# Folding the node mask into the last layer's relu in a four-layer graph network

## The chip, the cores and the metric

The kernel runs on one core of one Trainium2 chip. The metric is the device time of one execution in microseconds (us), as a median over runs. Five engines matter: TensorE (PE in the profile, with its weight loads as PEld), VectorE (DVE), ScalarE (ACT), GpSimd (POOL) and the DMA queue that SyncE (SP) feeds.

## What is computed

128 graphs of 128 nodes with 256 features pass four layers, each inside `x = layernorm(x + layer(x, adj))`. The layers are a hypergraph convolution with a hidden width of 512, a mean-aggregating layer, three stacked graph convolutions, and this last one, the only one whose code changes:

```python
def _L3_gnn_ref(x, a, kernel):
    t = jnp.einsum('bnm,bmf->bnf', a, x)
    out = jnp.einsum('bnf,fd->bnd', t, kernel)
    out = jax.nn.relu(out)
    mask = (jnp.sum((x != 0).astype(jnp.float32), axis=-1, keepdims=True) > 0).astype(jnp.float32)
    return out * mask
x = _layernorm(x + _L3_gnn_ref(x, adj, L3_gnn_kernel), axis=-1)
```

The mask has one number per node, 0 or 1.

## The kernel before, in words

The work unit is a pair of graphs: tiles are 128 partitions (nodes) by 2 x 256 elements. There are 64 pairs. The kernel is a software pipeline: `LAG` gives each stage the iteration in which it works, so that iteration n does, among others, stages R and P (layer one) of pair n-1, XAB and AXB (layer two) of pair n-2, Ax2, H1, H1W, H2 (layer three) of pair n-3, H2W, AP3, Ax3 and TK (end of layer three, and layer four) of pair n-4, and F (mask, last norm, store) of pair n-5. Each engine has its own hand-written order of operations in its function `body(n, k)`, and engines meet through counting semaphores alone. Iterations 0 to 2 are a written-out fill, and the last five drain the pipeline.

Products are made of three terms (hi x hi, hi x lo, lo x hi), so each operand is split in a rounded part (`_hi`, a copy on ScalarE, line 541) and a rest (`_lo`, a subtraction on VectorE, line 802, or on GpSimd, lines 1180 and 1188).

Names that the text uses:

- R writes the first layer's hidden values to PSUM; ScalarE's `relu_r` (line 565) makes `r_f`, `round_r` (541) `r_hi`, GpSimd's `low_r` (1188) `r_lo`; `square_r`, `add_squares` make `sq`, its halves and their sum. `copy_A` and `low_A` split the adjacency.
- A norm is `summed` (n_s), `stats` (n_st, 810), `mean_var` (n_mv, 815), `root` on ScalarE (n_std, 555), `invert` (n_rstd, 828), `shift` (n_shift, 832) and `apply` on ScalarE (560, two instructions, one per graph). The first norm is applied on VectorE instead (line 842). n1 to n4 are the norms of the four layers.
- `h_mean`, `h_var`, `h_veps`, `h_std`, `h_rstd` are the inner norm of layer one, and `p_f` (940) its result, which the matmuls of GP read.
- `x2c` (1265) is the second layer's result plus a bias, for the sum of the third (1108); `BH` (1207) serves the next pair's G; `h_lo` (1180) belongs to H1 and, later in the iteration, to H2.
- TK writes the last layer's product to PSUM bank 2. XAB of the next iteration writes the same bank, so TensorE waits there for `tk_relu` (line 379).
- F: VectorE counts the nonzero elements of `x3` and makes `mask` (1071, 1075). ScalarE has made `tk = relu(psum)` at the end of the iteration before (791, one 128x512 instruction). GpSimd multiplies `n4.s = tk * mask` first in its iteration (1246), and after `low_r`, `add_squares` and `low_A` adds `x3` (1254). VectorE's stats of n4 (line 1122) wait for that sum.

Of the kernel before, what the change touches and what calls it, by code (L numbers as in the profile page):

```python
# [7 lines left out]
ALU = mybir.AluOpType  # L8
ACT = mybir.ActivationFunctionType
# [8 lines left out]
           R=1, P=1, GP=1,  # L18
# [3 lines left out]
           F=5)  # L22
# [8 lines left out]
def build(nc, x, adjT, w1T, w2T, wab, v1, v2, v3, wk, columns, rows, eye, out):  # L31
    NP, C, GP_, D = x.shape
# [5 lines left out]
    with ExitStack() as ctx:  # L38
# [6 lines left out]
        def sem(name):  # L45
            return ctx.enter_context(nc.semaphore(name))
# [50 lines left out]
        x3 = sb("x3", [2, D])  # L97
# [51 lines left out]
        h1_relu, h1_hi, h1_lo, h1w_out = (sem(s) for s in ("h1_relu", "h1_hi", "h1_lo", "h1w_out"))  # L149
        h2_relu, h2_hi, h2_lo, h2w_hi, h2w_lo = (sem(s) for s in ("h2_relu", "h2_hi", "h2_lo", "h2w_hi", "h2w_lo"))  # L150
        x3_nz, mask_made = sem("x3_nz"), sem("mask_made")
        tk_masked = sem("tk_masked")
        ax3_hi, ax3_lo, tk_relu = sem("ax3_hi"), sem("ax3_lo"), sem("tk_relu")

        def begun(pair):

            return pair >= 0

        def upto(pair):

            return min(pair, NP - 1) + 1
# [5 lines left out]
        def active(stage, n):  # L167
            return 0 <= n - LAG[stage] < NP
# [25 lines left out]
        def bc(ap, shape, axis):  # L194
            return ap.unsqueeze(axis).to_broadcast(shape)
# [343 lines left out]
        def _(act):  # L539
# [44 lines left out]
            def round_r(n, k, h):  # L584
                p = n - 1
                act.wait_ge(r_relu[h], upto(p))
                if begun(p - 1):
                    act.wait_ge(pe_did["P"], upto(p - 1))
                copy(r_s[0][:, 2 * h:2 * h + 2], r_f[:, 2 * h:2 * h + 2]).then_inc(r_hi[h], 1)

            def square_r(n, k):
                p = n - 1
                act.wait_ge(r_relu[1], upto(p))
                if begun(p - 1):
                    act.wait_ge(sq_half, upto(p - 1))
                act.activation(sq[:], r_f[:], ACT.Square).then_inc(sq_made, 1)
# [104 lines left out]
            def body(n, k):  # L701
                if first(n, 4):
                    act.wait_ge(v_lo, 4)
                if active("x2", n):
                    p = n - 3
                    if begun(p - 1):
                        act.wait_ge(pe_did["Ax2"], upto(p - 1))
                        act.wait_ge(x2c_made, upto(p - 1))
                    apply(n2, p, x2)
                if active("R", n):  # L710
                    relu_r(n, k, 0)
                    relu_r(n, k, 1)
                if active("xT", n):
                    split_x1T(n, k)
                if active("R", n):
                    round_r(n, k, 0)
                if active("H2W", n):
                    split_hi("H2W", h2w, h2w_hi, n - 4, pe_did["AP3"])
                if active("R", n):
                    round_r(n, k, 1)  # L720
                if active("Ax2", n):
                    split_hi("Ax2", ax2, ax2_hi, n - 3, pe_did["H1"])
                if active("R", n):
                    square_r(n, k)
                    copy_A(n, k)
                if active("prep", n):
                    weight_column(n, k)
                if active("XAB", n):
                    out_XAB(n, k)
                if active("H1", n):  # L730
                    p = n - 3
                    act.wait_ge(pe_did["H1"], upto(p))
                    if begun(p - 1):
                        act.wait_ge(h1_lo, upto(p - 1))
                    relu_out("H1", 0, h1_f, c1_c)
                    relu_out("H1", 1, h1_f, c1_c).then_inc(h1_relu, 1)
                    act.wait_ge(h1_relu, upto(p))
                    if begun(p - 1):
                        act.wait_ge(pe_did["H1W"], upto(p - 1))
                    copy(h1_s[0][:], h1_f[:]).then_inc(h1_hi, 1)  # L740
                if active("AP3", n):
                    p = n - 4
                    root(n3, p)
                    if begun(p - 1):
                        act.wait_ge(pe_did["Ax3"], upto(p - 1))
                        act.wait_ge(n4.summed, upto(p - 1))
                        act.wait_ge(x3_nz, upto(p - 1))
                    apply(n3, p, x3)
                if active("F", n):
                    root(n4, n - 5)  # L750
                if active("P", n):
                    square_mean(n, k)
                if active("Tr", n):
                    copy_GT(n, k)
                if active("P", n):
                    root_h(n, k)
                if active("H1W", n):
                    p = n - 3
                    act.wait_ge(pe_did["H1W"], upto(p))
                    if begun(p - 1):  # L760
                        act.wait_ge(pe_did["H2"], upto(p - 1))
                    copy(h1w[:].rearrange("p g d -> p (g d)"),
                         psum[:, BANK["H1W"], 0:2 * D]).then_inc(h1w_out, 1)
                if active("Ax3", n):
                    split_hi("Ax3", ax3, ax3_hi, n - 4, pe_did["TK"])
                if active("Gx", n):
                    split_gx(n, k)
                if active("F", n):
                    p = n - 5
                    if p >= 2:  # L770
                        act.wait_ge(stored[p % 2], 16 * (p // 2))
                    apply(n4, p, x4[(k - 5) % 2])
                if active("H2", n):
                    p = n - 3
                    act.wait_ge(pe_did["H2"], upto(p))
                    if begun(p - 1):
                        act.wait_ge(h2_lo, upto(p - 1))
                    relu_out("H2", 0, h2_f, c2_c)
                    relu_out("H2", 1, h2_f, c2_c).then_inc(h2_relu, 1)
                    act.wait_ge(h2_relu, upto(p))  # L780
                    if begun(p - 1):
                        act.wait_ge(pe_did["H2W"], upto(p - 1))
                    copy(h2_s[0][:], h2_f[:]).then_inc(h2_hi, 1)
                if active("AXB", n):
                    root(n2, n - 2)
                if active("TK", n):
                    p = n - 4
                    act.wait_ge(pe_did["TK"], upto(p))
                    if begun(p - 1):
                        act.wait_ge(tk_masked, upto(p - 1))  # L790
                    act.activation(tk[:].rearrange("p g d -> p (g d)"), psum[:, BANK["TK"], 0:2 * D],  # L791
                                   ACT.Relu).then_inc(tk_relu, 1)
                if active("GP", n):
                    root(n1, n - 1)

# [382 lines left out]
        def _(pool):  # L1178
# [60 lines left out]
            def body(n, k):  # L1239
                if active("F", n):  # L1240
                    p = n - 5
                    pool.wait_ge(tk_relu, upto(p))
                    pool.wait_ge(mask_made, upto(p))
                    if begun(p - 1):
                        pool.wait_ge(n4.done, upto(p - 1))
                    pool.tensor_tensor(n4.s[:], tk[:], bc(mask[:], [C, 2, D], 2), ALU.mult).then_inc(tk_masked, 1)  # L1246
                if active("R", n):
                    low_r(n, k, 0)
                    low_r(n, k, 1)
                    add_squares(n, k)  # L1250
                    low_A(n, k)
                if active("F", n):
                    pool.wait_ge(tk_masked, upto(n - 5))
                    pool.tensor_tensor(n4.s[:], n4.s[:], x3[:], ALU.add).then_inc(n4.summed, 1)  # L1254
                if active("H1", n):
                    pool.wait_ge(h1_hi, upto(n - 3))
                    lo(h1_s, h1_f[:], h1_lo)
                if active("prep", n):
                    make_BH(n, k)
                if active("x2", n):  # L1260
                    p = n - 3
                    pool.wait_ge(n2.done, upto(p))
                    if begun(p - 2):
                        pool.wait_ge(n3.summed, upto(p - 2))
                    pool.tensor_tensor(x2c[(k - 3) % 2][:], x2[:], bc(c3_b, [C, 2, D], 1),
                                       ALU.add).then_inc(x2c_made, 1)
                if active("GP", n):
                    make_xb(n, k)
                if active("H2", n):
                    pool.wait_ge(h2_hi, upto(n - 3))  # L1270
                    lo(h2_s, h2_f[:], h2_lo)
# [44 lines left out]
```

## Time and profile before

| | |
|---|---|
| median of 3 runs | 1463.44 us (1463.33 to 1463.59) |
| the profiled execution's own time | 1463.48 us |
| its span, first to last instruction | 1461.7 us |
| granted TensorE clock, mean | 0.991 |
| busy share: PE, DVE, ACT, POOL | 97%, 74%, 72%, 58% |

A row of the timeline gives the start in us from the span's start, the duration in us, the engine, the line, the operation, what it writes and reads, and in brackets how long its engine sat idle before it and what ended that. Instructions of one kind that follow each other are merged ("x2"), and their duration is then from the first start to the last end. Neighbouring instructions of one engine overlap by about 0.05 to 0.1 us. Matmul ends are modelled, so a PE that looks busy without a break can still lose time between starts.

### The profile page before, as it was taken

How to read it: one execution, taken by the hardware profiler on the slowest of the kernel's cores; microseconds unless marked ns; L12 is line 12 of the kernel's file. 1: busy time of each engine (PE TensorE's matmuls, PEld its weight loads, DVE VectorE, ACT ScalarE, POOL GpSimd, SP SyncE). 2: the span in 40 equal slices, each digit the busy share in tenths (PEclk: the TensorE clock that was granted, in tenths of full speed). 3: DMA queues.
4: the chain of work that ended last, by engine and by line, in shares of the span. 5: the costliest groups of instructions: out<-in, count | busy, mean ns of one | idle time of the engine just before them, and what ended most of it. 6: DMA issues, size and time to landing. Idle time of an engine off the chain costs nothing. (4 is left out here: it accounts for less than half of the span.)

```text
span 1461.7 us, 33281 instructions
## 1 busy us (share of the span) xinstructions
PE 1416.2 (97%) x10896; PEld 1353.8 (93%) x10896; DVE 1080.4 (74%) x3744; ACT 1056.8 (72%) x2442; POOL 851.7 (58%) x776
## 2 busy tenths in 40 slices
PE   7899999999999999999999999999999999999974
PEld 6799999999999999999999999999999999999973
DVE  6667777777777777777777777777777777777663
ACT  4577777778777777777777777777777777777863
POOL 4565565565566566566566566566566566566542
PEclk9999999999999999999999999999999999999997
DMA  4001101101101101101101101101100100110000
GB/s 135 23 12 37 38 19 37 38 19 37 37 20 37 38 19 37 38 19 37 38 20 37 38 19 37 38 24 32 38 26 30 38 28 29 37 30 16 15 16 22
DMA packets 29946, 47.04 MB, mean 32 GB/s; under 512 B 3408, under 2 KB 12240, under 8 KB 29776
## 3 DMA queue, kind: packets, MB, share of 16 engines
q1 hardware_dynamic: 29776, 44.91, 9.8%
q8 instruction: 89, 1.46, 0.4%
q14 instruction: 81, 0.66, 0.2%
HBM read 28.12 MB, written 16.78 MB: 31 GB/s over the span
## 5 line engine op out<-in xcount | busy, mean ns | idle before, releaser
L1180 POOL TENSOR_TENSOR h_lo<-h_f,h_hi 128x512 fp32r<-128x512 f32 x128 | 166.2, 1298 | 373.4 <-ACT h_hi L541 373.4
L560 ACT ACTIVATE x<-n_s,n_shift,n_rstd 128x256 f32<-128x256 f32 x384 | 208.4, 590 | 101.0 <-DVE n_shift L832 101.0
L810 DVE BATCH_NORM_STATS2 n_st<-n_s 128x6 f32<-128x256 f32 x512 | 188.1, 409 | 7.6 <-POOL n_s L1254 5.2
L555 ACT ACTIVATE n_std<-n_mv,eps_c 128x2 f32<-128x2 f32 x256 | 74.7, 292 | 158.3 <-DVE n_mv L815 158.2
L1188 POOL TENSOR_TENSOR r_lo<-r_f,r_hi 128x512 fp32r<-128x512 f32 x128 | 163.5, 1299 | 36.6 <-ACT r_hi L541 36.4
L1246 POOL TENSOR_TENSOR n_s<-tk,mask 128x512 f32<-128x512 f32 x64 | 66.7, 1042 | 165.7 <-issue 150.4
L254 PE MATMUL psum<-v_hi,h_hi 128*128 128x256 f32 x512 | 148.9, 291 | 5.0 <-issue 5.0
L254 PE MATMUL psum<-A_f,x 128*128 128x128 f32 x1024 | 142.1, 282 | 5.4 <-ACT x L560 4.8
L254 PE MATMUL psum<-w2c_hi,r_hi 128*128 128x258 f32 x512 | 145.9, 285 | 0.5 <-POOL r_lo L1188 0.5
L254 PE MATMUL psum<-w2c_hi,r_lo 128*128 128x258 f32 x512 | 146.0, 285 | 0.0
L254 PE MATMUL psum<-w2c_lo,r_hi 128*128 128x258 f32 x512 | 144.8, 283 | 0.0
L254 PE MATMUL psum<-v_hi,h_lo 128*128 128x256 f32 x512 | 144.1, 282 | 0.0
L254 PE MATMUL psum<-v_lo,h_hi 128*128 128x256 f32 x512 | 144.0, 281 | 0.0
L254 PE MATMUL psum<-gx_hi,w1T_hi 128*128 128x256 f32 x512 | 143.9, 281 | 0.0
L254 PE MATMUL psum<-gx_hi,w1T_lo 128*128 128x256 f32 x512 | 143.3, 280 | 0.0
L254 PE MATMUL psum<-gx_lo,w1T_hi 128*128 128x256 f32 x512 | 143.3, 280 | 0.0
L565 ACT ACTIVATE h_f<-psum,columns 128x256 f32<-128x256 f32 x256 | 107.7, 473 | 48.9 <-PE psum L254 48.9
L254 PEld LDWEIGHTS psum<-A_f,x 128*128 128x128 f32 x1024 | 126.0, 193 | 8.1 <-ACT x L560 5.4
L1108 DVE TENSOR_TENSOR n_s<-psum,x2c 128x512 f32<-128x512 f32 x64 | 44.3, 692 | 87.0 <-PE psum L254 87.0
L254 PE MATMUL psum<-wab_hi,x1T_hi 128*128 128x512 f32 x256 | 106.8, 417 | 0.0
L802 DVE TENSOR_TENSOR ax_lo<-psum,ax_hi 128x512 fp32r<-128x512 f32 x128 | 87.8, 686 | 25.3 <-ACT ax_hi L541 25.3
L565 ACT ACTIVATE r_f<-psum,columns 128x256 f32<-128x256 f32 x256 | 99.1, 463 | 3.9 <-PE psum L254 3.9
(141 smaller groups left out, 5044.1 us busy)
## 6 DMA issues: line engine op xcount, KB each, us to landing
x_in<-x_in_dram SPq DMA_DIRECT2D x64, 256.0 KB, 3.0
out<-x SPq DMA_DIRECT2D x64, 256.0 KB, 2.0
at_in<-adjT SPq DMA_DIRECT2D x64, 128.0 KB, 2.3
x<-v_in SPq DMA_DIRECT2D x3, 256.0 KB, 5.8
n_s<-w2T_in SPq DMA_DIRECT2D x2, 256.0 KB, 3.7
r_f<-w1T_in SPq DMA_DIRECT2D x2, 256.0 KB, 4.7
h_f<-wab_in SPq DMA_DIRECT2D x2, 256.0 KB, 6.0
rows<-rows_in SPq DMA_DIRECT2D x1, 256.0 KB, 6.1
```

The source lines that it names most:

```text
L254: return pe.matmul(o, a, b, start=start, stop=stop)
L555: act.activation(nm.std[:], nm.mv[:, :, 1], ACT.Sqrt, bias=eps_c[:, 0:1]).then_inc(nm.rooted, 1)
L560: last = act.activation(dst[:, g, :], nm.s[:, g, :], ACT.Identity, scale=nm.rstd[:, g:g + 1], bias=nm.shift[:, g:g + 1])
L565: return act.activation(dst[:, m].rearrange("p g c -> p (g c)"), psum[:, BANK[stage] + extra, (m % 2) * 2 * C:(m % 2 + 1) * 2 * C], ACT.Re ...
L802: return dve.tensor_tensor(dst[1][:], src, f(dst[0][:]), ALU.subtract).then_inc(signal, 1)
L810: last = dve.bn_stats(nm.st[:, g, :], nm.s[:, g, :])
L1108: dve.tensor_tensor(n3.s[:].rearrange("p g d -> p (g d)"), flat(BANK["AP3"]), x2c[(k - 4) % 2][:].rearrange("p g d -> p (g d)"), ALU.add). ...
L1180: return pool.tensor_tensor(dst[1][:], src, f(dst[0][:]), ALU.subtract).then_inc(signal, 1)
L1188: pool.tensor_tensor(r_s[1][:, half], r_f[:, half], f(r_s[0][:, half]), ALU.subtract).then_inc(r_lo[h], 1)
L1246: pool.tensor_tensor(n4.s[:], tk[:], bc(mask[:], [C, 2, D], 2), ALU.mult).then_inc(tk_masked, 1)
```

## The change

ScalarE's relu of TK moves from the end of iteration n-1 to iteration n, between the split of `x1T` and that of `h2w`. It becomes two instructions, one per graph, each with the mask column as its `scale`, and waits for the mask as well. To make room in the written order, `round_r` of the first half moves behind the split of `h2w`, and that of the second half behind the split of `ax2`. GpSimd's multiplication is gone; its addition `n4.s = tk + x3` takes that place at the head of the iteration. The semaphore `tk_masked` is gone; what protected `tk` from being overwritten is now `n4.summed`.

```diff
@@ ScalarE, body @@
                 if active("xT", n):
                     split_x1T(n, k)
-                if active("R", n):
-                    round_r(n, k, 0)
+                if active("F", n):
+                    p = n - 5
+                    act.wait_ge(pe_did["TK"], upto(p))
+                    act.wait_ge(mask_made, upto(p))
+                    if begun(p - 1):
+                        act.wait_ge(n4.summed, upto(p - 1))
+                    for g in range(2):
+                        last = act.activation(tk[:, g, :], psum[:, BANK["TK"], g * D:(g + 1) * D], ACT.Relu,
+                                              scale=mask[:, g:g + 1])
+                    last.then_inc(tk_relu, 1)
                 if active("H2W", n):
                     split_hi("H2W", h2w, h2w_hi, n - 4, pe_did["AP3"])
                 if active("R", n):
-                    round_r(n, k, 1)
+                    round_r(n, k, 0)
                 if active("Ax2", n):
                     split_hi("Ax2", ax2, ax2_hi, n - 3, pe_did["H1"])
                 if active("R", n):
+                    round_r(n, k, 1)
                     square_r(n, k)
                     copy_A(n, k)
@@ ScalarE, body, near the end @@
-                if active("TK", n):
-                    p = n - 4
-                    act.wait_ge(pe_did["TK"], upto(p))
-                    if begun(p - 1):
-                        act.wait_ge(tk_masked, upto(p - 1))
-                    act.activation(tk[:].rearrange("p g d -> p (g d)"), psum[:, BANK["TK"], 0:2 * D],
-                                   ACT.Relu).then_inc(tk_relu, 1)
@@ GpSimd, body @@
                     pool.wait_ge(tk_relu, upto(p))
-                    pool.wait_ge(mask_made, upto(p))
                     if begun(p - 1):
                         pool.wait_ge(n4.done, upto(p - 1))
-                    pool.tensor_tensor(n4.s[:], tk[:], bc(mask[:], [C, 2, D], 2), ALU.mult).then_inc(tk_masked, 1)
+                    pool.tensor_tensor(n4.s[:], tk[:], x3[:], ALU.add).then_inc(n4.summed, 1)
                 if active("R", n):
                     low_r(n, k, 0)
                     low_r(n, k, 1)
                     add_squares(n, k)
                     low_A(n, k)
-                if active("F", n):
-                    pool.wait_ge(tk_masked, upto(n - 5))
-                    pool.tensor_tensor(n4.s[:], n4.s[:], x3[:], ALU.add).then_inc(n4.summed, 1)
```

## Rows read from the trace of the kernel before

**Rows 1.** The page, part 1: busy time of each engine, share, instructions.

```profile
PE 1416.2 (97%) x10896; PEld 1353.8 (93%) x10896; DVE 1080.4 (74%) x3744; ACT 1056.8 (72%) x2442; POOL 851.7 (58%) x776
```

**Rows 2.** Timeline of PE around Ax3, Gx, GP and H2, iteration 3, then a later one.

```profile
66.82 0.61 PE L254 MATMUL psum<-GT,x_in 128*128 128x128 f32 x4
67.27 1.03 PE L254 MATMUL psum<-p_f,GT 128*128 128x256 f32 x4
...
719.64 1.14 PE L254 MATMUL psum<-A_f,x 128*128 128x128 f32 x8
720.62 1.06 PE L254 MATMUL psum<-GT,x_in 128*128 128x128 f32 x8
721.61 1.13 PE L254 MATMUL psum<-p_f,GT 128*128 128x256 f32 x4
```

**Rows 3.** Timeline of DVE and ACT: from the n3 shift to p_f, and n1's variance.

```profile
717.39 0.97 DVE L832 SCALAR_TENSOR_TENSOR n_shift<-n_mv,n_rstd 128x2 f32<-128x2 f32 x1
...
718.48 1.09 ACT L560 ACTIVATE x<-n_s,n_shift,n_rstd 128x256 f32<-128x256 f32 x2 [1.60 <-DVE n_shift L832]
...
719.67 0.15 ACT L623 ACTIVATE h_mean<-psum 128x2 f32<-128x2 f32 x1
...
719.85 0.16 DVE L921 SCALAR_TENSOR_TENSOR h_var<-psum,h_mean 128x2 f32<-128x2 f32 x1 [1.49 <-ACT h_mean L623]
...
720.68 0.87 DVE L940 SCALAR_TENSOR_TENSOR p_f<-psum,h_rstd,betaW 128x256 f32<-128x256 f32 x2
...
726.43 0.23 DVE L815 BATCH_NORM_AGGREGATE n_mv<-n_st 128x2 f32<-128x6 f32 x2
```

**Rows 4.** Timeline of ACT: one iteration's head, and the next one's start.

```profile
704.86 0.30 ACT L555 ACTIVATE n_std<-n_mv,eps_c 128x2 f32<-128x2 f32 x1 [0.19 <-DVE n_mv L815]
705.06 1.08 ACT L560 ACTIVATE x<-n_s,n_shift,n_rstd 128x256 f32<-128x256 f32 x2
706.04 1.54 ACT L565 ACTIVATE r_f<-psum,columns 128x256 f32<-128x256 f32 x4
707.47 0.60 ACT L541 ACTIVATE x1T_hi<-psum 128x512 fp32r<-128x512 f32 x1
707.95 0.64 ACT L541 ACTIVATE r_hi<-r_f 128x512 fp32r<-128x512 f32 x1
708.47 0.61 ACT L541 ACTIVATE h2w_hi<-psum 128x512 fp32r<-128x512 f32 x1
...
712.07 0.60 ACT L541 ACTIVATE xbw_hi<-psum 128x512 fp32r<-128x512 f32 x1 [0.33 <-PE psum L254]
...
713.49 0.84 ACT L565 ACTIVATE h_f<-psum,columns 128x256 f32<-128x256 f32 x2 [0.33 <-PE psum L254]
...
726.69 0.30 ACT L555 ACTIVATE n_std<-n_mv,eps_c 128x2 f32<-128x2 f32 x1 [0.20 <-DVE n_mv L815]
```

**Rows 5.** Timeline of POOL, from its first idle stretch to x2c.

```profile
707.21 1.04 POOL L1246 TENSOR_TENSOR n_s<-tk,mask 128x512 f32<-128x512 f32 x1 [2.50 <-issue]
708.67 2.55 POOL L1188 TENSOR_TENSOR r_lo<-r_f,r_hi 128x512 fp32r<-128x512 f32 x2 [0.41 <-ACT r_hi L541]
711.18 1.34 POOL L1194 TENSOR_TENSOR sq<-sq 128x512 f32<-128x512 f32 x1
...
713.98 1.30 POOL L1254 TENSOR_TENSOR n_s<-n_s,x 128x512 f32<-128x512 f32 x1
...
716.48 0.63 POOL L1207 TENSOR_TENSOR BH<-HT,be_inv 128x256 f32<-128x256 f32 x1
717.05 1.30 POOL L1265 TENSOR_TENSOR x2c<-x,rows 128x512 f32<-128x512 f32 x1
```

**Rows 6.** Timeline of DVE: the same shift of norm n2, POOL idle.

```profile
704.74 0.14 DVE L832 SCALAR_TENSOR_TENSOR n_shift<-n_mv,n_rstd 128x2 f32<-128x2 f32 x1
```

**Rows 7.** Timeline of DVE (ax_lo) and PE: first matmuls of XAB, H1, AP3 and P.

```profile
710.12 0.69 DVE L802 TENSOR_TENSOR ax_lo<-psum,ax_hi 128x512 fp32r<-128x512 f32 x1 [0.32 <-ACT ax_hi L541]
...
708.98 0.48 PE L254 MATMUL psum<-wab_hi,x1T_hi 128*128 128x512 f32 x1
...
711.87 0.28 PE L254 MATMUL psum<-ax_hi,v_hi 128*128 128x256 f32 x1
...
713.28 0.28 PE L254 MATMUL psum<-h2w_hi,A_hi 128*128 128x256 f32 x1
...
713.99 0.28 PE L254 MATMUL psum<-w2c_hi,r_hi 128*128 128x258 f32 x1
```

**Rows 8.** Timeline of the drain: the last pair's relu, mask, sum and stats.

```profile
1453.16 0.60 ACT L791 ACTIVATE tk<-psum 128x512 f32<-128x512 f32 x1 [2.79 <-PE psum L254]
1453.84 1.04 POOL L1246 TENSOR_TENSOR n_s<-tk,mask 128x512 f32<-128x512 f32 x1 [12.98 <-ACT tk L791]
1454.95 1.26 POOL L1254 TENSOR_TENSOR n_s<-n_s,x 128x512 f32<-128x512 f32 x1
1456.25 0.75 DVE L810 BATCH_NORM_STATS2 n_st<-n_s 128x6 f32<-128x256 f32 x2 [5.25 <-POOL n_s L1254]
```

**Rows 9.** Groups of instructions (busy us, mean ns of one): ACT copies without column operands.

```profile
L541 ACT ACTIVATE GT<-psum 128x256 f32<-128x256 f32 x64 | 23.5, 367 | 5.1 <-PE psum L303 4.8
```

More of the change, by code:

```diff
@@ L151, in build @@
         x3_nz, mask_made = sem("x3_nz"), sem("mask_made")
-        tk_masked = sem("tk_masked")
         ax3_hi, ax3_lo, tk_relu = sem("ax3_hi"), sem("ax3_lo"), sem("tk_relu")
```

## The prediction, made before the changed kernel ran

> **What bounds the kernel now.** The busy shares come first: PE 97%, POOL 58% [rows 1]. Read alone, they say that TensorE is the bound and that work moved among the others is free. But the ends of matmuls are modelled, so the starts have to be read. In iteration 3, where p_f was early, the four matmuls of GP took 1.03 us; in a later iteration they take 1.13 [rows 2]. The eight matmuls of Gx start 0.99 us before GP there; the four shown at 66.82 need 0.45, so eight need 0.90 [rows 2]. GP therefore loses 0.09 before and 0.10 after its first matmul, 0.19 us in an iteration, and Ax3 at 719.64 is 0.98 before Gx where eight such matmuls need 0.90: another 0.08 [rows 2]. What GP waited for is p_f: it ended at 720.68 + 0.87 = 721.55, GP began at 721.61 [rows 2, 3]. So some 0.27 us of each iteration are a wait, and something other than TensorE sets the pace.
>
> The timelines of the other engines show what. Start at VectorE's shift of norm n3, which ends at 718.36. ScalarE's apply waits for it (718.48), then h_mean (719.67), VectorE's h_var waits for that (719.85), then p_f (720.68) [rows 3]. From p_f on VectorE has no idle time before any of its instructions up to the mean and variance of n1, which end at 726.66 [rows 3]; ScalarE's n_std waits for them (726.69, or 704.86 an iteration earlier) [rows 4]. From 704.86 ScalarE works without a break: apply, four r_f, x1T_hi, the first r_hi, which ends at 708.59. GpSimd waited for that one: r_lo at 708.67, and then works without a break down to x2c, 717.05 to 718.35 [rows 4, 5]. And the shift of n3, begun at 717.39, takes 0.97 us for two elements and ends at 718.36, 0.01 after x2c, while the same operation of n2, at a time when GpSimd is idle, takes 0.14 [rows 3, 5, 6]. So x2c holds the shift up, and the circle is closed: 726.69 - 704.86 = 21.83 us, with no TensorE step in it. Each iteration lasts as long as this ring. **What lengthens the ring lengthens the kernel one for one**; what lies beside it is free.
>
> **The change, part by part.**
>
> *The multiplication goes.* 64 x 1.04 us leave GpSimd, but the instruction ran at 707.21 and ended at 708.25, 0.41 before r_lo, which waited for ScalarE [rows 5]. It is beside the ring: gain 0. The cover is ScalarE's own work up to r_hi.
>
> *The old relu goes* from ScalarE's place before n_std. n_std waited 0.19 us for VectorE behind it [rows 4]: gain 0.
>
> *The new relus.* They start where r_hi started, 707.95 [rows 4]. No row has a relu with a column as its scale alone. The nearest are relus from PSUM of the same size with a column as bias: a pair (h_f) takes 0.84 us; the four r_f in 1.54, so a pair of them about 0.82 [rows 4]. The bounds: a copy of 256 elements without any column has 0.367 us [rows 9], which in a pair, less an overlap of 0.1, is 0.63; the pair of applies with two column operands took 1.08 [rows 4]. I take 0.83, so they end at 708.78 (708.58 to 709.03).
>
> *The addition* moves to GpSimd's head and waits for the relus. With the 0.08 that r_lo needed behind r_hi, it starts at 708.86, and with it the run of work that ends in x2c. That run has the same members as before (addition, two r_lo, two sums of squares, A_lo, h_lo, BH), only in another order, so x2c starts as much later as the run: 708.86 - 708.67 = **0.19 us** (bounds -0.01 and 0.44) [rows 5]. It starts at 717.24 instead of 717.05, still ahead of the shift at 717.39, which comes from VectorE's own work behind AP3 and does not move; the shift now ends 0.19 later. Nothing else in the run waits longer: r_hi starts behind two relus (0.73 of issue, the pair less an overlap) and h2w_hi (0.48), so at about 709.16, and ends at 709.80; GpSimd turns to it only at 708.86 + 1.25 = 710.11. The second r_hi ends some 1.0 later, at 710.81, and is wanted at 711.36.
>
> *The other waits behind ScalarE.* h2w_hi and ax2_hi are 0.2 later, each r_hi some 1.2. VectorE's ax_lo follows and ends at 711.01 instead of 710.81, where H1 starts at 711.87; h2w_lo ends before it, and AP3 starts at 713.28; the first r_lo ends at 711.4, and P starts at 713.99 [rows 7]: 0. square_r and what follows it come 0.7 later; two idle stretches of 0.33 us, before xbw_hi and before h_f, take that up [rows 4], and neither is in the ring: 0. If this cover were gone, h_hi and with it H1's h_lo on GpSimd would be late, which is in the ring. No DMA issue moves, and SP waits for the same n4.done.
>
> *XAB's bank.* TensorE's XAB starts at 708.98 [rows 7] and waits for tk_relu, before the change done 4 us earlier, now at 708.78; with the 0.06 that GP needed behind p_f this is 708.84. 0.14 remain: cost 0, but with applies' duration (709.03) it would be 0.1 an iteration, inside the same ring's delay.
>
> *Drain.* Once: before, relu 1453.16, sum started 1454.95 [rows 8]. After: 1453.16 + 0.83 + 0.08 = 1454.07. Gain 0.9 us.
>
> *Sum.* F runs from iteration 5, the full ring until iteration 63: 58 passes x 0.19 = 11.0, less 0.9: 10.1 us. The profiled execution took 1463.48, 0.04 over the median of the runs, so **1473.6 us**. Bounds: 58 x -0.01 gives 1462.0, 58 x 0.44 gives 1488.1.
>
> The Trainium skill, page "ScalarE: Activation LUTs", section on the instruction's timing, prices an instruction with immediate operands at 186 ns + 0.833 ns per element, each column operand at 93 ns more, and the overlap of neighbours at 93 ns. By it a relu here is an estimate of 0.49 us, the pair 0.89, the delay 0.25 and the total 1477 us. The rows of r_f and h_f have a smaller price for the same shape, and I stay with them.
>
> **The rivals.**
>
> *A, the shift slips through (faster).* The point that decides is whether x2c still starts before the shift asks at 717.39. My estimate leaves 0.15 us; another 0.15 on GpSimd, say 0.04 each from VectorE operations that now fall on other boundaries of GpSimd's run (the sum of squares takes 1.34 against 1.30 of its neighbours [rows 5]) plus a slower pair of relus, is enough. Then the shift waits for BH alone, takes less than 0.2 instead of 0.97, and the ring is 0.8 shorter in that pass. TensorE becomes the bound and can give back at most the 0.27 of its waits: 58 x 0.27 + 0.9 = 16.6, 1447 us. But after such a pass the chain, and x2c with it, come earlier, and the shift is caught again; so a part of the passes gain, and I put it at a third to a half, about 0.1 each: 1463.5 - 5.8 - 0.9 = 1457 us. Against it: the members of the run are the same, and no row shows GpSimd varying by 0.15.
>
> The skill's page "SBUF — State Buffer", section "Who interferes with whom", has the rule behind this: a VectorE instruction with two SBUF inputs and a GpSimd instruction that reads SBUF exclude each other for the whole length of whichever came first. The 0.97 against 0.14 agree with it. It says nothing of who comes next when GpSimd's instructions stand back to back, which is what rival A hangs on.
>
> *B, the relu costs what an apply costs (slower still).* 0.44 x 58 less 0.9: 1488 us. For it: a scale column may cost more than a bias column. Against: that price is of two columns, read from SBUF.
>
> *C, no change.* Some member of the ring has slack that the rows hide (the order of additions costs nothing, or a relu costs what a copy does), and only the drain counts: 1462.6 us. Against: no idle time on any hop.
>
> **How the numbers follow.** The forecast has 0.70, with 1469 to 1478 for itself (0.10 to 0.26 a pass); A 0.12, B 0.07, C 0.11. The likeliest gives 1473.6. The range takes in C and the upper part between forecast and B: 1461.5 to 1481; outside are A and B, 0.19. What this kernel's measurement can tell from no change is about 0.2%, 2.9 us. Faster is A, 0.12; same is C, 0.11; slower is the forecast and B, 0.77.
>
> **What would show it.** Right: in the changed kernel's timeline the pair of relus takes 0.8 to 0.9 right behind x1T_hi; GpSimd's run starts 4.0 us after n_std where it was 3.8; x2c starts before the n3 shift, which lasts some 1.15 us instead of 0.97 and still ends with x2c; n_std repeats every 22.0 us; GP's distance to Gx stays 0.99 and its four matmuls 1.13. Wrong: a shift of n3 below 0.5 us (A); a pair of 1.0 or more, with XAB waiting (B); an iteration of 21.8 with the relus where I put them (C), which would mean that the ring is not what sets the pace.

## The result, and the profile after

| | before | changed |
|---|---|---|
| median | 1463.51 us | 1475.75 us |
| lowest, highest of 4 runs | 1463.33, 1464.87 | 1475.21, 1477.07 |
| span of the profiled execution | 1461.7 us | 1473.4 us |

The changed kernel is slower: ratio 1.0083, 95% interval 1.0065 to 1.0100, 12.2 us. The forecast was 1473.6 us, with 1469 to 1478 for itself. The shown iteration is no exception: over 54 iterations of the full pipeline, from one start of GpSimd's first instruction to the next, the mean is 22.06 us, before 21.85.

The page of the changed kernel, part 1 (busy time, share, instructions), misleads if it is read alone: TensorE's busy time grew by 11.9 us without a single new matmul, and GpSimd lost 67 us of work.

```profile
PE 1428.1 (97%) x10896; PEld 1356.8 (92%) x10896; DVE 1092.1 (74%) x3744; ACT 1065.3 (72%) x2506; POOL 784.7 (53%) x712
```

The timeline of ScalarE in one iteration of the changed kernel, and its next start, answers to [rows 4]:

```profile
665.42 0.29 ACT L554 ACTIVATE n_std<-n_mv,eps_c 128x2 f32<-128x2 f32 x1 [0.68 <-DVE n_mv L816]
665.63 1.08 ACT L559 ACTIVATE x<-n_s,n_shift,n_rstd 128x256 f32<-128x256 f32 x2
666.61 1.54 ACT L564 ACTIVATE r_f<-psum,columns 128x256 f32<-128x256 f32 x4
668.04 0.60 ACT L540 ACTIVATE x1T_hi<-psum 128x512 fp32r<-128x512 f32 x1
668.52 0.85 ACT L721 ACTIVATE tk<-psum,mask 128x256 f32<-128x256 f32 x2
669.23 0.63 ACT L540 ACTIVATE h2w_hi<-psum 128x512 fp32r<-128x512 f32 x1
...
672.88 0.64 ACT L540 ACTIVATE xbw_hi<-psum 128x512 fp32r<-128x512 f32 x1
...
674.06 0.84 ACT L564 ACTIVATE h_f<-psum,columns 128x256 f32<-128x256 f32 x2
...
687.47 0.29 ACT L554 ACTIVATE n_std<-n_mv,eps_c 128x2 f32<-128x2 f32 x1 [0.68 <-DVE n_mv L816]
```

Up to x1T_hi nothing has changed against n_std (2.62 us, before 2.61). The pair of relus ends at 669.37. The iteration is 687.47 - 665.42 = 22.05 us instead of 21.83. The 0.68 us of idle time before n_std is the old relu's place: leaving it gained nothing, because n_std waits for VectorE.

The timeline of GpSimd in the same iteration, which answers to [rows 5]:

```profile
669.45 1.29 POOL L1246 TENSOR_TENSOR n_s<-tk,x 128x512 f32<-128x512 f32 x1 [4.17 <-ACT tk L721]
670.70 2.61 POOL L1189 TENSOR_TENSOR r_lo<-r_f,r_hi 128x512 fp32r<-128x512 f32 x2
673.27 1.27 POOL L1195 TENSOR_TENSOR sq<-sq 128x512 f32<-128x512 f32 x1
...
677.27 0.61 POOL L1208 TENSOR_TENSOR BH<-HT,be_inv 128x256 f32<-128x256 f32 x1
677.84 1.28 POOL L1262 TENSOR_TENSOR x2c<-x,rows 128x512 f32<-128x512 f32 x1
```

The run that ends in x2c starts 4.03 us after n_std, before 3.81: 0.22 later. It has lost its multiplication and is no shorter, because that never belonged to it. x2c is 8.39 us behind the run's start, before 8.38. One detail is new: the pair of r_lo takes 2.61 instead of 2.55 and the sum of squares 1.27 instead of 1.34. VectorE's HT now meets the first r_lo and ends behind it, and the second r_lo is the longer one; before, it met the second r_lo, and the sum of squares was the longer one. That the 0.06 belongs to the instruction behind the meeting fits these rows, but no run was made to show it.

The timeline of VectorE, which answers to [rows 3]:

```profile
677.99 1.15 DVE L833 SCALAR_TENSOR_TENSOR n_shift<-n_mv,n_rstd 128x2 f32<-128x2 f32 x1
680.63 0.16 DVE L922 SCALAR_TENSOR_TENSOR h_var<-psum,h_mean 128x2 f32<-128x2 f32 x1 [1.49 <-ACT h_mean L622]
...
681.45 0.88 DVE L941 SCALAR_TENSOR_TENSOR p_f<-psum,h_rstd,betaW 128x256 f32<-128x256 f32 x2
```

The shift takes 1.15 instead of 0.97 and ends at 679.14, 0.02 behind x2c. That is the sign that the prediction named. And TensorE, as in [rows 2]:

```profile
680.04 0.28 PE L253 MATMUL psum<-v_lo,h_hi 128*128 128x256 f32 x1
680.16 0.28 PE L253 MATMUL psum<-v_hi,h_lo 128*128 128x256 f32 x1
680.41 1.16 PE L253 MATMUL psum<-A_f,x 128*128 128x128 f32 x8
681.40 1.06 PE L253 MATMUL psum<-GT,x_in 128*128 128x128 f32 x8
682.38 1.13 PE L253 MATMUL psum<-p_f,GT 128*128 128x256 f32 x4
```

p_f ended at 682.33 and GP began at 682.38; 0.98 from Gx to GP and 1.13 for GP are as before, within 0.01. The largest part of the additional time stands before Ax3, whose operand x3 is made behind the late shift: Ax3 starts 0.25 after the last matmul of H1W, where neighbours are 0.12 apart and where it was 0.11 before.

In the drain the last pair, timeline of all engines, which answers to [rows 8], has 2.21 us from relu to stats instead of 3.09: 0.88 gained, once. By the rows the sum is then 58 x 0.22 less 0.88, 11.9 us; the medians are 12.2 apart.

```profile
1465.77 0.84 ACT L721 ACTIVATE tk<-psum,mask 128x256 f32<-128x256 f32 x2 [2.79 <-PE psum L253]
1466.68 1.26 POOL L1246 TENSOR_TENSOR n_s<-tk,x 128x512 f32<-128x512 f32 x1 [14.34 <-ACT tk L721]
1467.98 0.75 DVE L811 BATCH_NORM_STATS2 n_st<-n_s 128x6 f32<-128x256 f32 x2 [4.37 <-POOL n_s L1246]
```

### The profile page after: what moved, and what is told of

Same layout as the page of the kernel before. It is cut to its first block and busy times, and to the rows that moved or that the text cites. A ratio compares the mean times of both kernels' runs of the same rounds, so it can differ in the third digit from the quotient of the medians.

```text
span 1473.4 us, 33281 instructions
## 1 busy us (share of the span) xinstructions
PE 1428.1 (97%) x10896; PEld 1356.8 (92%) x10896; DVE 1092.1 (74%) x3744; ACT 1065.3 (72%) x2506; POOL 784.7 (53%) x712
## 5 line engine op out<-in xcount | busy, mean ns | idle before, releaser
L1246 POOL TENSOR_TENSOR n_s<-tk,x 128x512 f32<-128x512 f32 x64 | 82.4, 1288 | 270.4 <-ACT tk L721 270.4
L1189 POOL TENSOR_TENSOR r_lo<-r_f,r_hi 128x512 fp32r<-128x512 f32 x128 | 167.0, 1327 | 12.6 <-ACT r_hi L540 12.6
L253 PEld LDWEIGHTS psum<-v_hi,h_hi 128*128 128x128 f32 x512 | 96.9, 189 | 5.6 <-issue 5.6
```

Source lines behind the costliest of these rows:

```text
L253: return pe.matmul(o, a, b, start=start, stop=stop)
L1189: pool.tensor_tensor(r_s[1][:, half], r_f[:, half], f(r_s[0][:, half]), ALU.subtract).then_inc(r_lo[h], 1)
L1246: pool.tensor_tensor(n4.s[:], tk[:], x3[:], ALU.add).then_inc(n4.summed, 1)
```

## The experiments

Times are medians; each was compared with the kernel before on the same chip, whose medians were 1463.36 us for after_wait, before_wait, one_relu and sum_back, 1462.44 for the two kernels with two waits, two_plain_relus and relus_between, and 1463.83 for the last two. The changed kernel was not run again on these chips, so a distance to it, or between kernels of different chips, is the difference of their distances to the kernel before.

### Cutting the ring at x2c, with and without the change

Both kernels get the same lines:

```diff
                 if active("x2", n):
                     p = n - 3
                     pool.wait_ge(n2.done, upto(p))
+                    if begun(n - 4):
+                        pool.wait_ge(n3.shifted, upto(n - 4))
```

> The changed kernel, but GpSimd waits for the n3 shift before it starts x2c, so that the two no longer meet. Ring theory (the iteration lasts as long as the ring n_std, apply, r_f, relus, GpSimd's run, x2c, n3 shift, p_f): the shift falls from 1.16 to 0.2 us or less, GP's and Ax3's waits of some 0.27 us vanish, an iteration falls from 22.05 to about 21.56 us and the total from 1475.7 to about 1447 us. Rival 1 (the relus on ScalarE make the operands of TensorE late, or the bank of XAB is waited for): the extra wait can't help, 1475 to 1480 us. Rival 2 (TensorE is the bound and 12 us are its own slower matmuls): 1475 us.

> The kernel before, with the same wait of x2c for the n3 shift, and nothing of the change. Ring theory: the ring of the kernel before is cut at the same point, the shift falls from 0.97 to 0.2 us or less, an iteration from 21.84 to about 21.56 us, the total from 1463.5 to about 1447.5 us; it ends within 2 us of the changed kernel with the wait, since both are then bound by TensorE. Rivals 1 and 2: 1463 us or slightly more, and 12 us ahead of the changed kernel with the wait.

Measured: changed kernel with the wait 1466.25 us, ratio 1.0019 (1.0007 to 1.0031); kernel before with it 1465.80, ratio 1.0018 (1.0008 to 1.0027). The change's 12 us are gone, and the two are equal within their noise, as only the ring theory has it. But neither is at 1447: both expectations missed, by 18 to 19 us. The timeline of VectorE in the changed kernel with the wait says why:

```profile
673.11 0.13 DVE L833 SCALAR_TENSOR_TENSOR n_shift<-n_mv,n_rstd 128x2 f32<-128x2 f32 x1
674.72 0.16 DVE L922 SCALAR_TENSOR_TENSOR h_var<-psum,h_mean 128x2 f32<-128x2 f32 x1 [1.48 <-ACT h_mean L622]
674.92 1.00 DVE L925 SCALAR_TENSOR_TENSOR h_veps<-h_var,eps_c 128x2 f32<-128x2 f32 x1
```

and that of GpSimd beside it:

```profile
673.37 1.29 POOL L1264 TENSOR_TENSOR x2c<-x,rows 128x512 f32<-128x512 f32 x1 [0.36 <-issue]
674.62 1.28 POOL L1216 TENSOR_TENSOR xb<-x_in,b2half 128x512 f32<-128x512 f32 x1
```

The shift is down from 1.15 to 0.13, but the next instruction of VectorE with two inputs in SBUF, h_veps, now comes while xb runs, and takes 1.00 instead of 0.16; it ends at 675.92, xb at 675.90. The wait was passed on: of the 1.02 us gained at the shift, h_veps gave back 0.84, and the 0.18 left, times 58, is 10 us, near the 9 by which this kernel is ahead of the changed one. The kernel before gains 0.84 at its shift (0.97 to 0.13) and loses as much at h_veps (0.99 for 0.16), so it gains nothing. And xb, unlike x2c before, no longer depends on when the relus end, since x2c now waits for the shift: from n_std to the shift it is 12.55 us in both kernels (660.56 to 673.11, and 660.31 to 672.86), and GpSimd's idle time before x2c is 0.36 us with the change and 0.57 without it. That is why the change cost nothing here.

### Cutting it twice

```diff
                 if begun(p - 1):
                     pool.wait_ge(n1.summed, upto(p - 1))
+                if begun(n - 5):
+                    pool.wait_ge(n4.shifted, upto(n - 5))
                 pool.tensor_tensor(xb[:], x_in[:, (k - 1) % RING], bc(b2half[:], [C, 2, D], 1),
```

> The changed kernel with x2c waiting for the n3 shift, and xb waiting for the n4 shift. With the first wait alone the lock only moved: h_veps met xb and took 1.00 us instead of 0.16, and an iteration stayed at 21.85. Ring theory: with both meetings gone h_veps takes 0.16, the n4 shift 0.14, p_f ends some 0.8 us earlier, TensorE becomes the bound with an iteration of about 21.56 us, and the total is about 1447 us. Rival (TensorE or ScalarE itself needs 21.8 us): 1463 to 1466 us again, with h_veps short.

> The kernel before with the same two waits. Ring theory: 21.56 us an iteration, about 1448 us, within 2 us of the changed kernel with two waits, whose drain is 0.9 us shorter: the change itself then costs nothing. Rival: 1463 to 1466 us; or, if the change costs time outside the ring, a difference of several us between the two.

Measured: 1446.94 us, ratio 0.9891 (0.9877 to 0.9906), and 1446.71 us, ratio 0.9891 (0.9875 to 0.9908). Both beat the kernel before by 15.5 us or more and so the changed kernel by some 28, and the change costs nothing once the ring is cut. The timeline of VectorE in the changed kernel with two waits:

```profile
667.27 0.13 DVE L833 SCALAR_TENSOR_TENSOR n_shift<-n_mv,n_rstd 128x2 f32<-128x2 f32 x1
...
669.08 0.16 DVE L925 SCALAR_TENSOR_TENSOR h_veps<-h_var,eps_c 128x2 f32<-128x2 f32 x1
...
669.71 0.88 DVE L941 SCALAR_TENSOR_TENSOR p_f<-psum,h_rstd,betaW 128x256 f32<-128x256 f32 x2
```

and of TensorE:

```profile
669.53 1.05 PE L253 MATMUL psum<-A_f,x 128*128 128x128 f32 x8
670.42 1.06 PE L253 MATMUL psum<-GT,x_in 128*128 128x128 f32 x8
671.31 1.03 PE L253 MATMUL psum<-p_f,GT 128*128 128x256 f32 x4
```

p_f is ready at 670.59, 0.72 before GP starts; from Ax3 to Gx and from Gx to GP it is 0.89 each, and GP takes 1.03, the figure of iteration 3 in [rows 2]. The iteration is 21.56 us in both kernels, as expected. With p_f early and the distances at their shortest, TensorE now sets the pace. A meeting that is left is harmless: the n2 shift now runs into h_lo of GpSimd, and ScalarE's apply waits for it, 0.26 us,

```profile
676.28 1.09 ACT L559 ACTIVATE x<-n_s,n_shift,n_rstd 128x256 f32<-128x256 f32 x2 [0.26 <-DVE n_shift L833]
```

without a wait on TensorE.

### The length of the relus

One plain relu of 128x512 in the new place:

```diff
-                    for g in range(2):
-                        last = act.activation(tk[:, g, :], psum[:, BANK["TK"], g * D:(g + 1) * D], ACT.Relu,
-                                              scale=mask[:, g:g + 1])
-                    last.then_inc(tk_relu, 1)
+                    act.activation(tk[:].rearrange("p g d -> p (g d)"), psum[:, BANK["TK"], 0:2 * D],
+                                   ACT.Relu).then_inc(tk_relu, 1)
```

> The changed kernel with one 128x512 relu in the new place in place of two of 128x256, and without the mask as scale; the multiplication by the mask is left out of the computation altogether. It ends 0.28 us earlier (0.58 against the pair's 0.86). Ring theory: x2c and the n3 shift end 0.28 us earlier, 58 passes x 0.28 = 16 us less than the changed kernel, about 1459.5 us, some 4 us under the kernel before. Rival 1, in the form that the order of the r_hi and h2w_hi copies costs the time: r_hi is still 0.95 us later than before, so most of the 12 us stays, 1471 to 1476 us.

Two relus without the column:

```diff
-                        last = act.activation(tk[:, g, :], psum[:, BANK["TK"], g * D:(g + 1) * D], ACT.Relu,
-                                              scale=mask[:, g:g + 1])
+                        last = act.activation(tk[:, g, :], psum[:, BANK["TK"], g * D:(g + 1) * D], ACT.Relu)
```

> The changed kernel with its two relus, but without the mask column as scale; the mask is left out of the computation. This prices the column. Two relus without a column should take about 0.27 + 0.38 = 0.65 us instead of 0.86. Ring theory: iteration 0.2 us shorter, 58 x 0.2 = 12 us less than the changed kernel, about 1464 us. Rival (the number of instructions or their place costs, not their length): 1474 to 1476 us.

Measured: 1462.22 us, ratio 0.9990 (0.9980 to 1.0000), and 1463.64 us, ratio 1.0005 (0.9996 to 1.0014). Everything else of the new order, the later copies included, is in both, and the 12 us are not. The queries for the tile tk (minimum, median and maximum of one instruction, in ns) give the prices. The changed kernel:

```profile
L721 ACT ACTIVATE tk<-psum,mask x128: 455/494/502, 95.0 to 1466.1; 128x256 f32<-128x256 f32 x128
```

Two plain relus:

```profile
L721 ACT ACTIVATE tk<-psum x128: 359/400/413, 94.9 to 1455.1; 128x256 f32<-128x256 f32 x128
```

One relu:

```profile
L720 ACT ACTIVATE tk<-psum x64: 578/612/617, 97.0 to 1454.1; 128x512 f32<-128x512 f32 x64
```

The mask column costs 0.094 us in each relu, twice 0.094 = 0.19 on the ring; 58 times that is 11 of the 12 us lost. The rest of the account fits: two plain relus take about as long as the r_hi that stood in their place (0.67 against 0.64). One plain relu took 0.61 where I had put 0.58, so it came out 1.1 us under the kernel before on its chip and not 4.

### The place of GpSimd's addition

```diff
-                if active("F", n):
-                    p = n - 5
-                    pool.wait_ge(tk_relu, upto(p))
-                    if begun(p - 1):
-                        pool.wait_ge(n4.done, upto(p - 1))
-                    pool.tensor_tensor(n4.s[:], tk[:], x3[:], ALU.add).then_inc(n4.summed, 1)
                 if active("R", n):
                     low_r(n, k, 0)
                     low_r(n, k, 1)
                     add_squares(n, k)
                     low_A(n, k)
+                if active("F", n):
+                    p = n - 5
+                    pool.wait_ge(tk_relu, upto(p))
+                    if begun(p - 1):
+                        pool.wait_ge(n4.done, upto(p - 1))
+                    pool.tensor_tensor(n4.s[:], tk[:], x3[:], ALU.add).then_inc(n4.summed, 1)
```

> The changed kernel with GpSimd's addition of x3 back in its old place behind A_lo; ScalarE is left as changed. r_lo then waits for r_hi, which ends at 6.77 us of the iteration, so GpSimd's run starts 1.2 us later than in the kernel before. Ring theory: x2c then starts behind the n3 shift's request and the shift waits for the shorter rest of h_lo, ending some 0.6 us earlier than in the kernel before; what is late next is the n4 shift, which meets xb (16.5 to 17.8 us) and holds p_f. So the total depends on that meeting: 1460 to 1467 us, under the changed kernel's 1475.7 though everything on GpSimd is later. Rival 1 (later operands cost the time): r_lo and what follows is later than in the changed kernel or equal, so 1476 us or more.

Measured: 1465.68 us, ratio 1.0011 (0.9999 to 1.0023). GpSimd's run starts 1.2 us later than in the kernel before (5.03 us after n_std) and still the total is 10 us under the changed kernel: what counts is what the shift meets. The timeline of VectorE:

```profile
674.35 0.26 DVE L833 SCALAR_TENSOR_TENSOR n_shift<-n_mv,n_rstd 128x2 f32<-128x2 f32 x1
...
676.87 0.79 DVE L833 SCALAR_TENSOR_TENSOR n_shift<-n_mv,n_rstd 128x2 f32<-128x2 f32 x1
677.58 0.87 DVE L941 SCALAR_TENSOR_TENSOR p_f<-psum,h_rstd,betaW 128x256 f32<-128x256 f32 x2
```

and of GpSimd:

```profile
673.30 1.29 POOL L1181 TENSOR_TENSOR h_lo<-h_f,h_hi 128x512 fp32r<-128x512 f32 x1
674.55 0.62 POOL L1208 TENSOR_TENSOR BH<-HT,be_inv 128x256 f32<-128x256 f32 x1
...
676.37 1.27 POOL L1216 TENSOR_TENSOR xb<-x_in,b2half 128x512 f32<-128x512 f32 x1
```

The n3 shift met the end of h_lo and ended 0.02 behind it, although BH was GpSimd's next and had been started at 674.55: here the waiting VectorE instruction got in between two of GpSimd's. The n4 shift met xb, 0.79 instead of 0.14, and p_f waited for it: the next meeting in line, as expected.

### The relus outside the ring, and a miss

```diff
+                if active("R", n):
+                    round_r(n, k, 0)
                 if active("F", n):
...
                     last.then_inc(tk_relu, 1)
+                if active("R", n):
+                    round_r(n, k, 1)
                 if active("H2W", n):
                     split_hi("H2W", h2w, h2w_hi, n - 4, pe_did["AP3"])
-                if active("R", n):
-                    round_r(n, k, 0)
                 if active("Ax2", n):
                     split_hi("Ax2", ax2, ax2_hi, n - 3, pe_did["H1"])
                 if active("R", n):
-                    round_r(n, k, 1)
                     square_r(n, k)
```

and GpSimd's addition behind the second `low_r`.

> The changed kernel with ScalarE's order x1T_hi, first r_hi, the two masked relus, second r_hi, h2w_hi, ax_hi, and GpSimd's addition behind the second r_lo. Nothing of the computation differs. The first r_hi and with it GpSimd's run start where they did in the kernel before; the relus end about 6.28 us after the start of R, where XAB wants its bank at 5.85. Ring theory: x2c starts and the n3 shift ends as in the kernel before, TensorE waits some 0.4 us at XAB in place of GP and Ax3, and the iteration stays at 21.84: 1462 to 1465 us, 11 us under the changed kernel. Rival (XAB's wait for its bank, or the load of two more relus on ScalarE, is what costs): 0.4 us x 58 more than the changed kernel or at least no less, 1475 to 1499 us.

Measured: 1497.74 us, ratio 1.0237 (1.0222 to 1.0252): a miss by 33 us. Among the waits of this kernel between 100 and 1400 us (total, times, longest, in us) is one of TensorE, in each of 58 iterations, that the kernel before doesn't have in that stretch:

```profile
PE psum L253 <- DVE Gd L883: 19.4, 58, 0.4
```

AP3 also waits for Gd, since it writes G's bank, and I had left that wait out. By the starts it costs 0.50 us: AP3's first matmul comes 0.62 behind H1's last, where neighbours are 0.12 apart, in the timeline of TensorE:

```profile
684.30 0.28 PE L253 MATMUL psum<-ax_hi,v_lo 128*128 128x256 f32 x1
684.92 0.36 PE L253 MATMUL psum<-h2w_hi,A_hi 128*128 128x256 f32 x1 [0.34 <-DVE Gd L883]
```

The timeline of VectorE, where Gd is made:

```profile
682.29 0.98 DVE L890 TENSOR_SCALAR HT<-at_in 128x256 f32<-128x256 f32 x1
...
683.76 0.69 DVE L899 TENSOR_SCALAR be<-ht_count 128x2 f32<-128x2 f32 x1
684.36 0.41 DVE L883 TENSOR_TENSOR Gd<-psum,dinv 128x256 f32<-128x256 f32 x1
```

and of GpSimd, where the addition now stands in HT's way (it ends at 683.12):

```profile
681.83 1.29 POOL L1250 TENSOR_TENSOR n_s<-tk,x 128x512 f32<-128x512 f32 x1
683.08 1.34 POOL L1196 TENSOR_TENSOR sq<-sq 128x512 f32<-128x512 f32 x1
```

Two more kernels put this reading to the test: the same with the two waits of GpSimd from above, and that one with the addition moved on behind `low_A`.

> relus_between (the relus between the two r_hi, the addition behind the second r_lo) with the two waits of GpSimd. relus_between took 22.41 us an iteration against an expected 21.84. Theory Gd: TensorE lost 0.28 us at XAB (bank) and another 0.50 at AP3, which also waits for Gd (it shares G's bank); Gd is late because HT met the addition on GpSimd (0.99 us instead of 0.57) and then be met the sum of squares. That doesn't go through x2c, so the two waits change nothing: 21.56 + 0.28 + 0.50 = 22.34 to 22.42 us an iteration, 1493 to 1498 us. Rival (the ring through x2c and the n3 shift is what relus_between is still bound by): with the waits it falls to 21.84 or less, 1463 us or less.

> The same with GpSimd's addition moved behind A_lo. Then GpSimd is idle from the end of the second r_lo (7.97) until sq is there (8.6), and HT, asked at 8.39, meets nobody. Theory Gd: HT takes about 0.2, Gd is ready at about 10.25 us, before AP3 wants it, and only XAB's wait for its bank is left, 0.28 us in an iteration that TensorE otherwise fills: 21.56 + 0.28 = 21.84, about 1463 us (1461 to 1466). Rival 1 (the late h2w_hi or ax_hi themselves hold AP3 or H1 up): AP3's 0.5 stays, 1493 us or more. Rival 2 (the bank wait is absorbed): 1447 us.

Measured: 1499.39 us, ratio 1.0247 (1.0230 to 1.0264), and 1466.06 us, ratio 1.0012 (1.0002 to 1.0021). The first is 1.4 us above the expected range, the second at the upper end of its own. The two waits change nothing (35.6 us over the kernel before, without them 35.3), so x2c and the n3 shift are not what binds there; moving one addition of 1.3 us, for whose result nothing on the way to AP3 waits, gives back 33 us. The timeline of VectorE in the second:

```profile
668.33 0.28 DVE L890 TENSOR_SCALAR HT<-at_in 128x256 f32<-128x256 f32 x1
...
669.10 0.76 DVE L899 TENSOR_SCALAR be<-ht_count 128x2 f32<-128x2 f32 x1
669.77 0.41 DVE L883 TENSOR_TENSOR Gd<-psum,dinv 128x256 f32<-128x256 f32 x1
```

HT takes 0.28, Gd ends at 670.18, and AP3 starts at 670.47 without a wait for it. In the timeline of TensorE XAB follows 1.10 behind Ax2's start, in the changed kernel with two waits 0.80 (658.06 to 658.86):

```profile
665.06 1.05 PE L253 MATMUL psum<-A_f,x 128*128 128x128 f32 x8
...
666.16 0.47 PE L253 MATMUL psum<-wab_hi,x1T_hi 128*128 128x512 f32 x1
```

The 0.30 is XAB's wait for its bank, expected at 0.28, and 58 x 0.30 = 17 of the 18 us by which this kernel stands over the changed kernel with two waits (2.2 over the kernel before on its chip, against 15.5 under).

## Why the prediction was right, point by point

- **What bounds the kernel: right, and shown.** The ring was read from the trace alone; the two-wait kernels cut it, and the iteration fell to where the prediction had TensorE's own pace (0.27 us less; 16.6 us, 1447 us), at 1446.9 and 1446.7.
- **The multiplication and the old relu, gain 0: right.** 67 us of GpSimd's work went, the run to x2c didn't shorten, and n_std's idle time grew from 0.20 to 0.68 in place of an earlier start.
- **The new relus, 0.83: 0.02 to 0.03 too low.** They took 0.85 and the delay was 0.22 by the rows instead of 0.19. By the 58 passes that is 1.2 to 1.7 us, and the forecast was 2.1 short of the median. The page "ScalarE: Activation LUTs" of the Trainium skill, section "What ACT_TABLE_LOAD costs", gives 93 ns for a column, and the estimate from it was 0.49 for a relu; the trace agrees with both, 94 ns and 0.49. For the pair the estimate was 0.89, and 0.85 was measured: the second relu started 0.36 after the first (668.88), so the two overlap by 0.13, where the page has 93 ns. So the page was right on the single terms, and the rows of r_f and h_f were nearer for the pair; the estimate of 1477 was 1.3 over, my 1473.6 was 2.1 under.
- **x2c still ahead of the shift (rival A): held** with 0.15 to spare: 677.84 against 677.99, as put. That is partly luck: the shift, which was said not to move, asks 12.57 us after n_std where it was 12.53, and x2c is as much later than put. That a waiting VectorE instruction does get in between two of GpSimd's, which the rival needs, was seen in sum_back.
- **XAB's bank, cost 0: held** here; between_sum_last is where it costs.
- **The cover behind ScalarE: held, but only just, and the sum was short.** The prediction let two idle stretches of 0.33 take up 0.7. Measured, xbw_hi starts 7.46 us after n_std (before 7.21) without any idle time left, and h_f 8.64 (before 8.63): the copy between them (673.36 to 674.01) ends 0.05 us before h_f starts. Behind it 0.44 us more is left before the ring is touched: h_hi ends at 675.57, and GpSimd turns to h_lo at 676.01.
- **The drain, 0.9: 0.88.**
- **Rivals B and C fell:** the pair took 0.85 and not 1.08, and no hop of the ring took up the delay: 0.22 us arrived at the shift's end and 0.22 at the next n_std.
- **The list of waits was incomplete.** AP3's wait for Gd, and HT's and be's meetings ahead of it, are in no step of the prediction. In this change they had room; in relus_between they cost 33 us.

## What to carry to other kernels

A busy share of 97% does not name the bound: compare the starts of the same group in an iteration where its operand was early, and follow the operand back. If the chain closes on itself an iteration later, whatever lengthens it costs that length times the number of iterations (here a pair of relus of 0.85 us in the place of a copy of 0.64), and work taken off an engine beside it is worth nothing while the chain stands. Where VectorE and GpSimd share the work, look at tiny VectorE instructions with long durations; the GpSimd instruction that ends together with one of them is the one to hold back, and after one is freed the next in line has to be looked at before the gain can be counted.

## What had not been expected

Moving one GpSimd addition by two places (behind add_squares and low_A) is worth up to 33 us here, 2% of the kernel, through a VectorE instruction that it holds up (HT 0.98 us in relus_between, 0.28 in between_sum_last).

The Trainium skill, page "SBUF — State Buffer", section "Who interferes with whom", says that VectorE's `tensor_scalar` can take part in such meetings too, beside instructions with two SBUF inputs. The traces agree: HT took 0.98 us behind a GpSimd instruction and 0.28 when GpSimd was idle, and be took 0.69 us for two elements, where mask, a `tensor_scalar` of the same size with GpSimd idle, took 0.17 (changed kernel, 667.47). The rule doesn't say who comes next; in sum_back it was the waiting VectorE instruction.

In the changed kernel the matmuls from AP3 to the first of `ones,sq` take 3.65 us (673.87 to 677.52), in the kernel before 3.60 (713.28 to 716.88). No wait shows there, and the cause is open.

And two added waits made the changed kernel 15.5 us faster than the kernel before, the best complete version without them, although GpSimd now stands idle for 0.55 and 1.12 us an iteration behind them.
